# Attention B's operands as pairs of fp16 pieces, its scales normalised on the chip, and the FFN weights kept in SBUF

## The reference

```python
w = (qw.astype(jnp.float32) - 8.0) * jnp.repeat(scales, 128, axis=0)   # int4 weights, scales of 128 rows
q = apply_rope(x @ w_q); k = apply_rope(x @ w_k); v = x @ w_v          # 32 heads of 128; 8 heads of k and v
scores = einsum('bhqd,bhkd->bhqk', q, k) / sqrt(128)                   # causal
ctx = einsum('bhqk,bhkd->bhqd', softmax(scores), v)
x = x + ctx @ w_o                                                      # w_o: 4096 x 512, int4 with scales
```

## Time and profile before

| | us |
|---|---|
| median of 3 runs | 1661.92 |
| lowest and highest | 1657.54, 1664.38 |
| the profiled execution | 1654.98 |
| its span, first to last instruction | 1653.2 |

### The profile page before, as it was taken

How to read it: one execution, slowest core, us unless ns; L and a number is a source line. 1 busy time by engine, 2 the same in 40 slices (tenths; PEclk the granted TensorE clock), 3 DMA queues, 4 the chain that set the end, 5 groups by cost and what they waited for, 6 DMA issues and landing times.

```text
span 1653.2 us, 25343 instructions
## 1 busy us (share of the span) xinstructions
PE 1537.8 (93%) x7932; PEld 928.9 (56%) x7932; DVE 1212.0 (73%) x2306; ACT 854.7 (52%) x1468; POOL 255.1 (15%) x174
## 2 busy tenths in 40 slices
PE   5689999999999997999999998999999999999979
PEld 3313333323233456777767776776766767767744
DVE  4388888888882586786886886885886877877764
ACT  2106766666677133554564564554564555645531
POOL 2102000000000221232122122132032122212020
PEclk9859999999999997999999999999999999999999
DMA  4992000000001341673763862862863854853631
GB/s 112 141 163 79 1 1 0 0 0 0 0 0 14 98 128 26 143 150 71 164 137 64 183 131 55 184 131 59 177 134 71 177 114 85 174 102 58 144 68 51
DMA packets 369511, 148.32 MB, mean 90 GB/s; under 512 B 323688, under 2 KB 341480, under 8 KB 369136
## 3 DMA queue, kind: packets, MB, share of 16 engines
q1 hardware_dynamic: 369392, 146.87, 43.4%
HBM read 61.33 MB, written 7.90 MB: 42 GB/s over the span
## 4 chain that ended last, share of the span: by engine, by line
PE 69%; DVE 15%; issue 5%; ACT 5%; DMA 4%; SPq 2%; ACTq 0%; POOL 0%; DVEq 0%
PE ps L1408 9%; PE ps L1190 9%; PE ps L1410 8%; PE ps L1409 8%; PE ps L1243 7%; PE ps L1229 6%; DVE hl L1026 4%; PE ps L1370 3%; PE ps L1489 3%; PE ps L1491 3%; PE ps L1490 3%; DVE nmb L1015 3%; DMA hlT<-hl 2%; DVE mx L818 2%; PE ps L1333 2%
## 5 line engine op out<-in xcount | busy, mean ns | idle before, releaser
L818 DVE TENSOR_REDUCE mx<-ps 128x1 f32<-128x512 f32 x512 | 327.7, 686 | 65.4 <-PE ps L1190 63.2
L665 ACT ACTIVATE x<-ps,nmb 128x128 f32<-128x128 f32 (+7 forms) x256 | 188.8, 743 | 287.9 <-DVE nmb L1015 287.9
L579 ACT ACTIVATE proj<-ps 128x1024 f32<-128x1024 f32 x256 | 248.4, 1021 | 124.5 <-PE ps L1229 123.6
L1026 DVE SCALAR_TENSOR_TENSOR hl<-x,rden,hl 128x128 f16<-128x128 f32 (+7 forms) x256 | 225.1, 879 | 33.1 <-ACT hl L673 22.2
L1190 PE MATMUL ps<-ks,qs 96*128 (+1 forms) x512 | 199.4, 413 | 33.2 <-DVE pieces L843 15.1
L673 ACT ACTIVATE hl<-x,rden 128x128 f16<-128x128 f32 (+7 forms) x256 | 184.2, 767 | 53.6 <-DVE rden L1022 52.0
L493 POOL TENSOR_TENSOR tmp<-tmp 128x640 f32<-128x640 f32 x64 | 100.4, 1569 | 701.6 <-DVE tmp L1011 701.6
L1015 DVE TENSOR_REDUCE nmb<-ps 128x1 f32<-128x128 f32 (+7 forms) x256 | 191.7, 749 | 3.5 <-PE ps L1472 3.4
L1408 PE MATMUL ps<-wh,xTh 128*128 128x256 f32 (+1 forms) x512 | 180.6, 353 | 0.0
L1409 PE MATMUL ps<-wl,xTh 128*128 128x256 f32 (+1 forms) x512 | 174.3, 341 | 0.0
L1410 PE MATMUL ps<-wh,xTl 128*128 128x256 f32 (+1 forms) x512 | 173.6, 339 | 0.0
(11 more groups left out here) (177 smaller groups left out, 2498.2 us busy)
## 6 DMA issues: line engine op xcount, KB each, us to landing
st<-in_L_attn_b_qw_q_dram SPq DMA_DIRECT2D x32, 256.0 KB, 3.1
scale<-n_L_attn_b_scales_q_dram SPq DMA_DIRECT2D x32, 256.0 KB, 3.5
st<-in_L_attn_b_qw_o_dram SPq DMA_DIRECT2D x32, 256.0 KB, 3.4
scale<-n_L_attn_b_scales_o_dram SPq DMA_DIRECT2D x32, 256.0 KB, 4.1
qs<-scratch SPq DMA_DIRECT2D x24, 256.0 KB, 8.4
scratch<-pieces SPq DMA_DIRECT2D x5, 768.0 KB, 13.2
xnat<-attn_a_hidden_state_dram SPq DMA_DIRECT2D x8, 256.0 KB, 4.6
x<-attn_a_hidden_state_dram SPq DMA_DIRECT2D x4, 512.0 KB, 18.8
```

The lines of the kernel that those rows point to most:

```text
L579: nc.scalar.activation(pbuf[:, e % 4, :].rearrange("p (b n) -> p b n", b=2), ps[:, b:b + 2, :], ACT.Exp, scale=float(HD) ** -0.5).then_inc ...
L665: nc.scalar.activation(pr[:, h, 0:n], flat(2 * (h % 2), n), ACT.Exp, bias=nmb[:, h:h + 1], accum_out=den[:, h:h + 1]).then_inc(s_eb, 1)
L818: nc.vector.tensor_reduce(mx[:, f, k // 2, k % 2:k % 2 + 1], ps[:, bank(k), :], AX.X, ALU.max).then_inc(s_mx, 1)
L1026: nc.vector.scalar_tensor_tensor(hl[:, h, n:2 * n], pr[:, h, 0:n], rden[:, h:h + 1], hl[:, h, 0:n], ALU.mult, ALU.subtract).then_inc(s_lo, 1)
```

## The change

x, the dequantised weights, q, k and the context become pairs of fp16 pieces. So that they stay in fp16's range, all scales (q, k, v, o) are divided by their group's largest one and multiplied by 2^12 on the chip, once (`normalise_scales`), and stored to DRAM; x is multiplied by 2^10 as it is copied. The group's maxima come back as two factors: factors[g, 0] is the scale of the exponentials and is multiplied on the negated maximum, factors[g, 1] is applied in `add`. The order of SBUF changes so that hlT0 has a tile of its own, fw stays untouched, and the second FFN reads it in place.

```diff
+XSCALE = 2.0 ** 10
+WSCALE = 2.0 ** 12
+HEADROOM = 2.0 ** 3
...
-            xTh, xTl = (scoped(mem, f"xT{c}", [P, KC, S], F32R) for c in "hl")
-            wh, wl = (scoped(mem, f"w{c}", [P, KC, BW], F32R) for c in "hl")
-            woh, wol = (scoped(mem, f"wo{c}", [P, R, D], F32R) for c in "hl")
+            xTh, xTl = (scoped(mem, f"xT{c}", [P, KC, S], F16) for c in "hl")
+            qTh, qTl = (scoped(mem, f"qT{c}", [P, R, P], F16) for c in "hl")
+            kTh, kTl = (scoped(mem, f"kT{c}", [P, S], F16) for c in "hl")
...
+            cTh, cTl = (scoped(mem, f"cT{c}", [P, R, P], F16) for c in "hl")
...
+            wh, wl = (scoped(mem, f"w{c}", [P, KC, BW], F16) for c in "hl")
+            woh, wol = (scoped(mem, f"wo{c}", [P, R, D], F16) for c in "hl")
...
+            hlT0 = scoped(mem, "hlT0", [P, R, 2 * (T - 1), P], F16)
...
-        hlT0 = fw[:, 0:R * (T - 1) * P].bitcast(F16).rearrange("p (h b n) -> p h b n", h=R, b=2 * (T - 1))
-        late = ffn_weights(st[:, 0:FW])
...
-            sp.dma_start(svT[:], sv_d.rearrange("c (g p) -> p c g", p=P), allow_slow_non_contiguous=True).then_inc(s_sv, 16)
...
+            for r0, n, (src, _), form in SCALES:
+                sp.dma_start(sn[r0:r0 + G, 0:n].rearrange("g (c n) -> g c n", c=KC),
+                             src.rearrange(form, g=G)).then_inc(s_sn, 16)
...
-            sp.dma_start(sv_n.rearrange("c (g p) -> p c g", p=P), svT[:], allow_slow_non_contiguous=True).then_inc(s_svs, 16)
-            sp.wait_ge(s_xr, 16 * 6)
-            sp.wait_ge(s_we, KC + 3)
-            sp.dma_start(fw_d, fw[:]).then_inc(s_fws, 16)
+            for i, (r0, n, (_, dst), form) in enumerate(SCALES):
+                sp.wait_ge(s_snn, 2 * i + 2)
+                sp.dma_start(dst.rearrange(form, g=G),
+                             sn[r0:r0 + G, 0:n].rearrange("g (c n) -> g c n", c=KC)).then_inc(s_sns, 16)
+                sp.dma_start(top_d[i:i + 1, :].rearrange("o g -> g o"), top[r0:r0 + G, 0:1],
+                             allow_slow_non_contiguous=True).then_inc(s_sns, 16)
+            sp.wait_ge(s_sns, 16 * 8)
+            sp.dma_start(tops[:].rearrange("p a g -> p (a g)"),
+                         top_d.rearrange("a g -> (a g)").partition_broadcast(P)).then_inc(s_top, 16)
...
-                if isinstance(g, int) and g == G - 1 and t == 4:
-                    sp.wait_ge(s_wld, G * R)
-                    sp.wait_ge(s_wlp, G * KC)
-                    sp.wait_ge(s_fws, 16)
-                    sp.dma_start(st[:, 0:FW], fw_d).then_inc(s_fw2, 16)
...
                 nc.scalar.activation(cTh[:].rearrange("p h n -> p (h n)"), ps[:, 5, :], ACT.Copy,
-                                     scale=sgv[:, 2, ds(g, 1)]).then_inc(s_ch_b, 1)
+                                     scale=1.0 / PSCALE).then_inc(s_ch_b, 1)
...
                     nc.scalar.activation(pr[:, h, 0:n], flat(2 * (h % 2), n), ACT.Exp, bias=nmb[:, h:h + 1],
-                                         accum_out=den[:, h:h + 1]).then_inc(s_eb, 1)
+                                         scale=factor[:, par, 0:1], accum_out=den[:, h:h + 1]).then_inc(s_eb, 1)
...
+            def normalise_scales():
+
+                dve.wait_ge(s_sn, 16 * 4)
+                for i, (r0, n, _, _) in enumerate(SCALES):
+                    rows = slice(r0, r0 + G)
+                    nc.vector.tensor_reduce(top[rows, 0:1], sn[rows, 0:n], AX.X, ALU.max,
+                                            apply_absolute_value=True).then_inc(s_snn, 1)
+                    dve.wait_ge(s_snn, 2 * i + 1)
+                    link(nc.vector.tensor_scalar(top[rows, 0:1], top[rows, 0:1], 1e-30, None, ALU.max))
+                    link(nc.vector.reciprocal(top[rows, 1:2], top[rows, 0:1]))
+                    nc.vector.tensor_scalar(sn[rows, 0:n], sn[rows, 0:n], top[rows, 1:2], WSCALE,
+                                            ALU.mult, ALU.mult).then_inc(s_snn, 1)
...
                         maxima(u + 2, f, 0, 6, in_ring)
-                    elif f == 1:
+                    elif f == 0:
+                        normalise_scales()
+                    else:
                         weight(KC - 1)
...
-            def maximum(u, h, n):
+            def maximum(u, h, n, par):
                 dve.wait_ge(s_sc, u * R + h + 1)
-                nc.vector.tensor_reduce(nmb[:, h:h + 1], flat(2 * (h % 2), n), AX.X, ALU.max, negate=True).then_inc(s_nb, 1)
+                nc.vector.tensor_reduce(nmr[:, h:h + 1], flat(2 * (h % 2), n), AX.X, ALU.max, negate=True).then_inc(s_mxb, 1)
+                dve.wait_ge(s_mxb, u * R + h + 1)
+                nc.vector.tensor_scalar(nmb[:, h:h + 1], nmr[:, h:h + 1], factor[:, par, 0:1], None,
+                                        ALU.mult).then_inc(s_nb, 1)
+
+            def group_factor(g, par):
+                nc.vector.tensor_copy(factor[:, par, :], factors[:, ds(g, 1), :].rearrange("p o a -> p (o a)")).then_inc(s_fcr, 1)
...
-                nc.vector.tensor_tensor(xnat[:, t, :], xnat[:, t, :], ps[:, 4, :], ALU.add).then_inc(s_xo, 1)
+                nc.vector.scalar_tensor_tensor(xnat[:, t, :], ps[:, 4, :], factor[:, par, 1:2], xnat[:, t, :],
+                                               ALU.mult, ALU.add).then_inc(s_xo, 1)
...
+                if t == T - 1 and not last:
+                    group_factor(g + 1, 1 - par)
```

More of the change, by code:

```diff
@@ L141, in build @@
             bo = scoped(mem, "bo", [P, D])
+            sn = scoped(mem, "sn", [P, KC * D])
         wo = xT[:, 0:2, :].rearrange("p a (b n) -> p (a b) n", b=2)
@@ L146, in build @@
         with ExitStack() as mem:
-            xTh, xTl = (scoped(mem, f"xT{c}", [P, KC, S], F32R) for c in "hl")
-            wh, wl = (scoped(mem, f"w{c}", [P, KC, BW], F32R) for c in "hl")
-            woh, wol = (scoped(mem, f"wo{c}", [P, R, D], F32R) for c in "hl")
+            xTh, xTl = (scoped(mem, f"xT{c}", [P, KC, S], F16) for c in "hl")
+            qTh, qTl = (scoped(mem, f"qT{c}", [P, R, P], F16) for c in "hl")
+            kTh, kTl = (scoped(mem, f"kT{c}", [P, S], F16) for c in "hl")
+            vh, vl = (scoped(mem, f"v{c}", [P, T + 2, P], F16) for c in "hl")
+            cTh, cTl = (scoped(mem, f"cT{c}", [P, R, P], F16) for c in "hl")
+            nmr = scoped(mem, "nmr", [P, R])
+            nmb = scoped(mem, "nmb", [P, R])
+            den = scoped(mem, "den", [P, R])
+            rden = scoped(mem, "rden", [P, R])
+            scoped(mem, "gap", [P, 3 * P * 2])
+            wh, wl = (scoped(mem, f"w{c}", [P, KC, BW], F16) for c in "hl")
+            woh, wol = (scoped(mem, f"wo{c}", [P, R, D], F16) for c in "hl")
             st = scoped(mem, "st", [P, KC * BW + R * D])
             scale = scoped(mem, "scale", [P, 2, BW])
-            qTh, qTl = (scoped(mem, f"qT{c}", [P, R, P], F32R) for c in "hl")
-            kTh, kTl = (scoped(mem, f"kT{c}", [P, S], F32R) for c in "hl")
-            vh, vl = (scoped(mem, f"v{c}", [P, T + 2, P], F16) for c in "hl")
-            cTh, cTl = (scoped(mem, f"cT{c}", [P, R, P], F32R) for c in "hl")
             cos = scoped(mem, "cosines", [P, T, HALF_D])
@@ L518, in _ @@
             steps(step, pool)
-            pool.wait_ge(s_fw2, 16)
-            add_base_bias(xnat, 3, late[3])
+            add_base_bias(xnat, 3, bb)
         @block.scalar
@@ L536, in tokens @@
                     nc.scalar.activation(dst, ps[:, turn_bank(phase, t), :].rearrange("p (k n) -> p k n", k=KC),
-                                         ACT.Copy).then_inc(s_xt, 1)
+                                         ACT.Copy, scale=XSCALE if phase == 2 else 1.0).then_inc(s_xt, 1)
             root(0, 0)
@@ L1063, in step @@
                     low(u - 1, 2, (one[1] + 1) * P)
-                maximum(u, 0, n)
+                if t == 0:
+                    dve.wait_ge(s_fcr, g + 1)
+                maximum(u, 0, n, par)
                 if exists(*one):
@@ L1069, in step @@
                     rope_sin(t2)
-                maximum(u, 1, n)
+                maximum(u, 1, n, par)
                 invert(u, 0)
@@ L1073, in step @@
                     values_low(u + 1, par if t < T - 1 else 1 - par, t2)
-                maximum(u, 2, n)
+                maximum(u, 2, n, par)
                 low(u, 0, n)
-                maximum(u, 3, n)
+                maximum(u, 3, n, par)
                 if not end:
@@ L1083, in step @@
                 if exists(*two):
-                    add(u - 2, two[1])
+                    add(u - 2, two[1], par if t >= 2 else 1 - par)
                 if exists(*one):
                     context_low(*one)
+                if t == T - 1 and not last:
+                    group_factor(g + 1, 1 - par)
             def final_statistics(*tiles):
@@ L1094, in _ @@
             link(nc.vector.tensor_copy(mask[:], mask32))
+            dve.wait_ge(s_top, 16)
+            nc.vector.scalar_tensor_tensor(factors[:, :, 0], tops[:, 0, :], SC_B / (HEADROOM * HEADROOM), tops[:, 1, :],
```

(12 more changed lines are left out.)

116 lines of the change are left out of this document (55 added, 61 removed).

## The result

| | us |
|---|---|
| the changed kernel, median of 16 runs | 1665.15 (1660.96 to 1668.97) |
| the kernel before, median of 16 runs beside them | 1657.57 (1653.33 to 1664.38) |
| ratio, with its 95% interval | 1.0043 (1.003 to 1.0056) |

That is 7.6 us slower. I had forecast 1697 us; 4 of the 32 us between are the kernel before itself, 1661.92 by the three runs that I started from and 1657.57 by the sixteen here. The execution profiled has a span of 1660.3 us, against 1653.2.

A forecast was written before the change was run, and what follows sets the result against it. PE was taken to set most steps of attention B, with DVE close behind and setting t=7. The sum was 1655 + 30 + 7 - 2 = 1690 us, or 1697 as a median of runs, range 1642 to 1714.

The forecast's parts named there:

- I take it to be held, because the nearest instruction in kind, place and size is: Attention B, head 1: POOL's 1.57 us rotary sum holds DVE's new 128x1 tensor_scalar; exponentials start 2.00 us after the maximum started.
- theory A: In attention B, POOL holds head 1's added instruction and DVE becomes the bound: 1697 us, range 1680 to 1715; chance 0.57.
- the forecast (+30): Steps of attention B: +3.7 us a group, +30 us in eight groups.
- rival 2: In attention B, one element a partition is not held: -15 us in the steps, 1652 us for the kernel; chance 0.28.
- The row that I leaned on: A 128x2 tensor_scalar behind the exponentials that meets POOL's sum takes 0.95 us instead of 0.17 and ends with POOL.
- The price of an instruction: Each added DVE multiplication between a maximum and its exponential, four a step, costs 0.26 us; low end 0.08.
- a sign: DVE's busy time in attention B was to rise by 50 us or more.
- What PE gains: fp16 matmuls in attention B start closer together than fp32r ones: 58 us in 64 steps, if nothing else binds.
- The 0.9 us of a step: PE's saving in each step of attention B from fp16 matmuls and fewer changes of type.
- the transfers that the change removes: Two element-by-element copies of scales_v and two 1.8 MB FFN copies, under compute: 2 us off, at most 5.
- Ahead of attention B: normalise_scales in attention A's last group delays PE: +7 us, between 0 and 12; less 2 for removed transfers.
- +35: The whole kernel: +30 us in attention B, +7 ahead of it, -2 for removed transfers.

The follow-up runs named there:

- one load, scales behind: The changed kernel with q's, k's and v's scales in one array with one load, and the scales normalised behind `normalise`; multiplications kept: 1636.3 us, ratio 0.9853.
- all three: The changed kernel with the factor put on q's pieces, one array and one load for q's, k's and v's scales, and scales normalised behind `normalise`: 1620.4 us, ratio 0.9756.

## Why the prediction was wrong

The lengths of the steps, by the distance between two `turn_b`, as means over the groups, in us:

| t | before | after | one load, scales behind | all three |
|---|---|---|---|---|
| 0 | 13.6 | 13.4 | 13.4 | 13.2 |
| 1 | 16.1 | 15.8 | 16.0 | 16.4 |
| 2 | 12.8 | 12.2 | 12.3 | 12.7 |
| 3 | 12.8 | 12.0 | 12.0 | 12.0 |
| 4 | 14.0 | 14.7 | 13.4 | 12.7 |
| 5 | 14.7 | 15.9 | 14.7 | 14.3 |
| 6 | 16.1 | 15.4 | 15.4 | 15.0 |
| 7 | 18.7 | 19.9 | 19.9 | 18.9 |
| stage | 931.7 | 934.3 | 917.5 | 902.6 |

**The step that failed** is "I take it to be held, because the nearest instruction in kind, place and size is". All of theory A's weight, 45 us between the forecast (+30) and rival 2 (-15), stood on it. The instruction was never held (212 to 215 ns, 256 times), and with one more element a partition it was, each of the 85 times that POOL was running. The row that I leaned on had 128x2, and the difference between one and two elements was just the one that counts. I had the exponentials of head 1 start 0.8 us (t=7) to 1.7 us (t=0) later for it; they start 0.25 later.

The Trainium skill (Vector Engine (DVE) Microarchitecture Reference, Performance modes), which I had cited for the odd count that is equal in source and destination, asks this of the most major dimension that is not of size one. An instruction of 128x1 has no such dimension, so I had stretched the rule to a case that it doesn't name. The traces here show no hold for one element. They do show one for two, and there the second instruction waits for the end of the first, as the Trainium skill (SBUF — State Buffer, Who interferes with whom) has it.

**The price of an instruction** was right: 0.26 us taken, 0.214 busy, and exp 0.25 us later than before. Its own pointer scale costs 0.09 us, where I took 0.06. What I had wrong is that nothing else on DVE would change: its busy time from 660 to 1590 us rose by 20.5 us and not by the 50 or more that I named as a sign, though the new instructions are busy for 54.7. A part of the rest is the inversions: they come later against POOL's sum, and the first instruction of each takes 27.5 us in all (L1043, from 630 to 1560 us) where it took 38.0 (L1019).

**What PE gains** was nearly right. In a stream of the changed kernel, the fp16 matmuls of 512 columns start 0.216 us apart and those of 256 columns 0.109:

```profile
1048.36 0.27 PE L1445 MATMUL ps<-wh,xTh 128*128 128x256 f16 x1
...
1049.67 0.38 PE L1445 MATMUL ps<-wh,xTh 128*128 128x512 f16 x1
...
1052.26 0.38 PE L1445 MATMUL ps<-kTh,qTh 128*128 128x512 f16 x1
```

That is (1049.67 - 1048.36)/12 and (1052.26 - 1049.67)/12. The 0.9 us of a step shows as 0.7 in t=2, 3 and 6, and PE's busy time fell by 48.7 us where I had 58.

**The steps** then go by rival 2, which I had at 0.28. It gave -15 us for the stage; without the slow loads it is 917.5 - 931.7 = -14.2. It said +1.1 for t=7 and +0.2 for t=5; measured +1.2 and 0.0. Its t=0 (-0.5) came out at -0.2, t=4 (+0.2) at -0.6, t=1 (-0.9) at -0.1, t=6 (-0.2) at -0.7. So the mechanism is right in t=7, and that the sum agrees within 1 us is in part luck, since errors of opposite sign cancel.

**What no rival had** is what the loads of the scales take back: 17 us by the stages with three loads and with one (934.3 - 917.2), 21 us by the ratios (1.0043 - 0.9913). It lies in t=4 and 5, which are 0.8 and 1.2 us longer than before in the changed kernel (before rounding). I had forecast 1.0 for each, so these two steps seem to bear the forecast out, but by luck: with one load they are 0.6 shorter and unchanged. I had priced the transfers that the change removes, the eight stores and the one load that it adds, and had put down nothing for loads that keep their sizes and only get another source. The runs with a gap and with k's array taken out show that it is the neighbourhood of sk_n and sv_n, since no instruction changes with a gap and v's landing falls from 4.8 to 3.6 or 3.7 us. One load instead of three is better still by 0.0054, 9 us. What in the memory makes the neighbours slow isn't settled. Whether those 9 us come from the fewer issues on the queue or from a disturbance that a gap leaves isn't either, but the run with q's, k's and o's scales from the inputs has all the issues and comes within 0.0015 of the single load (0.9928 and 0.9913, with overlapping intervals), which speaks for the disturbance.

**Ahead of attention B** I forecast +5, and the first `turn_b` came 4.9 late. The timelines of the last group of attention A, first where the row maxima are negated in the kernel before, then the changed kernel's answer to the earlier trace rows:

```profile
499.14 0.19 DVE L826 TENSOR_REDUCE nm<-mx 128x16 f32<-128x32 f32 x1
```

```profile
498.17 0.19 DVE L843 TENSOR_REDUCE nm<-mx 128x16 f32<-128x32 f32 x1
...
499.13 2.27 DVE L811 TENSOR_REDUCE top<-sn 8x1 f32<-8x2048 f32 x1
...
508.97 1.28 DVE L816 TENSOR_SCALAR sn<-sn,top 8x2048 f32<-8x2048 f32 x1
...
510.57 0.42 DVE L860 TENSOR_TENSOR pieces<-ps,rc 128x256 f32<-128x256 f32 x1
511.05 1.01 PE L1254 MATMUL ps<-identb,mparts 128*3 128x128 bf16 x8 [7.14 <-DVE pieces L860]
```

Normalising took 11.1 us (499.13 to 510.25; 11.7 forecast), and PE waited 7.14 (7 forecast). The way from the negated maxima to the first `turn_b` was 129.7 us before and is 135.6 in the changed kernel, so +5.9 by this count. The start itself varies: in the eight executions whose normalisation stands where the changed kernel has it, the first `turn_b` lies between 632.8 and 637.2 us, but the way to it only between 134.5 and 136.5. With the scales behind it is 127.8, and 126.3 with the single load as well, where the single load alone has 135.1. So the place gives 7.8. The single load adds 1.5 once the place is right, hardly more than executions differ by. A wait of DVE for v's scales just ahead of the stage may be that: it is 4.12 us with the scales behind, and the chain of that run goes through it:

```profile
586.24 3.21 SPq L419
589.97 6.19 DMA scale<-sv_n
596.18 0.97 DVE st L952
```

No run tests this reading.

So the forecast's +35 were +7.6: -14.2 for the operands with their multiplications, +17 for neighbouring arrays, +5 ahead of the stage, by the single executions that were profiled. Two errors partly cancel: 44 us too many in the stage, for the hold, 17 too few for the loads. Without the second the forecast would have been further off.

## What to carry to other kernels

An instruction that is sure to meet a GpSimd instruction is worth a look at how many elements a partition it has: here one was never held, and two waited for the end of the other each time. Small arrays that are read one after another, above all by broadcast, should lie apart or be one array with one load, and a change that only moves data to new arrays wants its loads' landings compared, not only their bytes. A gain on the engine that seems to be the bound is worth only what the second engine leaves: of PE's 49 us, 14 arrived, and 15 more came with two small things taken out between the maxima and the exponentials, an instruction on DVE and a pointer on ACT. The instruction alone had cost 4.5 us while PE was the bound. And the same stage in two executions can differ by 7 us, so a part of a few us wants several runs or a count from a nearby mark.
